# Causal linear attention with 64 heads of width 8: the product of running state and queries in 32 matmuls of two heads instead of 64 of one

## What is computed

```python
xn = _layernorm(x)
q = heads(xn @ Wq.T + bq); k = heads(xn @ Wk.T + bk); v = heads(xn @ Wv.T + bv)
be = jnp.exp(beta)
q = softmax(be * q, axis=-1)
k = softmax(be * k, axis=-1)
kv = jnp.cumsum(jnp.einsum('zsD,zsd->zsDd', k, v), axis=1)
kn = jnp.cumsum(k, axis=1)
num = jnp.einsum('zsD,zsDd->zsd', q, kv)
den = jnp.sum(q * kn, axis=-1, keepdims=True)
attn = (num / den) @ Wo.T + bo
ffn = fp8(clip(xn / input_scale)) * input_scale @ (weight_fp8 * weight_scale).T + bias
out = x + attn + ffn
```

## Time and profile before

| | us |
|---|---|
| median of 3 runs | 1386.97 |
| lowest and highest run | 1383.36 and 1387.37 |
| the profiled execution, device time | 1375.45 |
| its span, first to last instruction | 1373.7 |
| TensorE busy (matmul) | 1224.7 |
| TensorE busy (weight loads) | 731.5 |
| VectorE busy | 1024.7 |
| ScalarE busy | 577.5 |
| GpSimd busy | 321.5 |

### The profile page before, as it was taken

How to read it: one execution, slowest core, us unless ns; L and a number is a source line. 1 busy time by engine, 2 the same in 40 slices (tenths; PEclk the granted TensorE clock), 3 DMA queues, 4 the chain that set the end, 5 groups by cost and what they waited for, 6 DMA issues and landing times.

```text
span 1373.7 us, 81313 instructions
## 1 busy us (share of the span) xinstructions
PE 1224.7 (89%) x36322; PEld 731.5 (53%) x36322; DVE 1024.7 (75%) x2031; ACT 577.5 (42%) x1049; POOL 321.5 (23%) x590
## 2 busy tenths in 40 slices
PE   1569999998999999999999899999999999999995
PEld 1335555555555555555555555555555555555653
DVE  4667778877777887778777777877777877778872
ACT  1534344444444444444444344344344444344431
POOL 3132222222222222222222222221222222122210
PEclk8789999999999999999999999999999999999998
DMA  8022232323323333333333333233233333323321
GB/s 223 10 67 65 75 84 75 82 76 79 75 73 83 70 85 76 81 74 85 76 75 77 76 80 71 77 79 69 76 86 66 76 86 77 75 77 76 69 65 42
DMA packets 181142, 106.01 MB, mean 77 GB/s; under 512 B 120160, under 2 KB 153056, under 8 KB 180832
## 3 DMA queue, kind: packets, MB, share of 16 engines
q1 hardware_dynamic: 180112, 99.79, 30.3%
q10 hardware_dynamic: 720, 1.31, 0.6%
HBM read 40.20 MB, written 16.78 MB: 41 GB/s over the span
## 4 chain that ended last, share of the span: by engine, by line
PE 86%; issue 8%; DVE 2%; DMA 1%; SPq 1%; POOL 0%; ACT 0%; POOLq 0%; DVEq 0%; ACTq 0%
PE s_ps L888 10%; PE a_ps L985 7%; PE a_ps L1004 6%; PE a_ps L905 6%; PE k_ps L861 5%; PE vo_ps L861 5%; PE vo_ps L963 5%; PE vo_ps L863 4%; PE k_ps L865 4%; PE vo_ps L865 4%; PE k_ps L863 4%; PE vo_ps L872 4%; PE vo_ps L874 4%; PE vo_ps L876 4%; PE q_ps L863 4%
## 5 line engine op out<-in xcount | busy, mean ns | idle before, releaser
L507 ACT ACTIVATE q_heads<-qT,cst 128x512 f32<-128x512 f32 x256 | 164.0, 711 | 88.1 <-DVE qT L753 88.1
L400 POOL TENSOR_TENSOR y_sum<-y,y_magic 128x512 f32<-128x512 f32 x64 | 81.4, 1272 | 450.3 <-DVE y_magic L614 450.3
L659 DVE TENSOR_TENSOR att<-s_ps,cst 128x512 f32<-128x512 f32 x256 | 163.8, 681 | 2.1 <-PE s_ps L888 2.1
L393 POOL TENSOR_TENSOR x_split<-xn,x_split 128x512 f16<-128x512 f32 x64 | 74.0, 1157 | 370.6 <-ACT x_split L455 363.4
L498 ACT ACTIVATE q_e<-q_shift,q_exp_scale 128x512 f32<-128x512 f32 x64 | 46.2, 722 | 252.0 <-DVE q_shift L632 252.0
L888 PE MATMUL s_ps<-q_heads,kT 32*32 32x128 f32 x8192 | 148.3, 272 | 2.1 <-issue 1.2
L888 PEld LDWEIGHTS s_ps<-q_heads,kT 32*32 32x32 f32 x8192 | 113.6, 103 | 56.3 <-issue 56.3
L985 PE MATMUL a_ps<-st_seqs,q_heads 128*32 128x36 f32 x8192 | 99.3, 201 | 35.6 <-issue 33.9
L712 DVE TENSOR_TENSOR vp<-vo_ps,vp 128x512 f32<-128x512 f32 x64 | 44.3, 692 | 109.1 <-PE vo_ps L865 109.1
L985 PEld LDWEIGHTS a_ps<-st_seqs,q_heads 128*32 128x32 f32 x8192 | 89.1, 109 | 68.4 <-issue 66.1
L905 PE MATMUL a_ps<-vp,k_e 32*32 32x36 f32 x8064 | 115.0, 198 | 6.4 <-issue 6.3
(11 more groups left out here) (136 smaller groups left out, 2450.4 us busy)
## 6 DMA issues: line engine op xcount, KB each, us to landing
v_groups<-vp SPq DMA_DIRECT2D x1024, 18.0 KB, 2.4
x_in<-L_attn_x SPq DMA_DIRECT2D x64, 256.0 KB
x_res<-L_attn_x SPq DMA_DIRECT2D x64, 256.0 KB
out<-o_sb SPq DMA_DIRECT2D x64, 256.0 KB
w_own<-L_attn_Wk SPq DMA_DIRECT2D x1, 1024.0 KB, 11.4
w_own<-L_attn_Wq SPq DMA_DIRECT2D x1, 1024.0 KB, 13.5
w_own<-L_attn_Wv SPq DMA_DIRECT2D x1, 1024.0 KB, 15.2
att<-L_ffn_weight_fp SPq DMA_DIRECT2D x1, 1024.0 KB, 16.9
```

The costliest lines, as they stand in the source:

```text
L393: gp.tensor_tensor(x_split[:, 1, :], xn[:, :], x_split[:, 0, :], ALU.subtract)\
L400: gp.tensor_tensor(y_sum[:, :], y[:, :], y_magic[:, :], ALU.add).then_inc(ysum_ready, 1)
L507: last = sc.activation(q_heads[:, i.parity, :, j, :], qT[:, :, :], ACT.Copy, scale=head_mask[:, j:j + 1])
L659: v.tensor_tensor(att[:, c, :, :, :].rearrange("p g j s -> p (g j) s"), s_ps[:, DM * (c % 2):DM * (c % 2 + 1)].rearrange("p (h s) -> p h s ...
```

## The change

The inner loop over the four heads of a group takes two at a time. The weights are then 64 columns, two heads side by side, which lie next to each other in `q_heads`, and the result goes to 64 PSUM partitions. The moving operand, the accumulation and the place of every result are as before. The waits are as before too. A step has 32 calls on line 985 instead of 64, and they use two tiles of 64 columns in turn instead of four of 32.

```diff
                     for g in range(G):
-                        for j in range(J):
-                            mm(a_ps[TOK * j:TOK * (j + 1), a_col(g):a_col(g) + GW],
-                               q_heads[:, t.parity, g, j, :], st_seqs[:, t.parity, g, :, :],
+                        for j in range(0, J, 2):
+                            mm(a_ps[TOK * j:TOK * (j + 2), a_col(g):a_col(g) + GW],
+                               q_heads[:, t.parity, g, j:j + 2, :].rearrange("p j s -> p (j s)"),
+                               st_seqs[:, t.parity, g, :, :],
                                start=(g % (G // 2) == 0), stop=False, skip_group_check=True)
```

## The result

| | before | after |
|---|---|---|
| median of the runs side by side, us | 1385.16 (4 runs) | 1325.61 (4 runs) |
| lowest and highest | 1381.10 and 1387.37 | 1323.97 and 1328.23 |
| profiled execution, us | 1375.45 | 1327.04 |
| its span, us | 1373.7 | 1325.2 |
| its mean granted clock | 0.967 | 0.980 |

The ratio is 0.9579, 95% interval 0.9537 to 0.9621: 4.2% faster, where 1.0% was forecast.

The account below looks back on a forecast made before the run. The prediction took TensorE's own queue as the bound. From the profiled 1375.45 us, + 0.7 - 9.1 - 5.0 gave 1362.0 us, 1.0% less, or 1373.5 us carried over to the median; range 1344 to 1400.

Parts of the forecast that it names:

- my case: The whole kernel: 1.0% less time, 4 to 22 us less with terms at their ends; chance 0.56.
- Term 1: Inter product, line 985: half the calls on half the tiles leave array time unchanged at 1.12 us a step; 0.
- Term 2: Weight loads on line 985: 64-column loads stay hidden except the first of each step; +0.7 us, bounds 0 and +22.5.
- The slower rival: Line 985: the 64-column load takes a tile longer than its pass and becomes the bound; up to 1423 us, chance 0.20.
- Term 3: TensorE's issue stops fall in proportion to the 11.3% fewer instruction records; -9.1 us, bounds 0 and -33.9.
- Term 4: Inter product: part of its extra time, from reading beside other engines, goes as fewer streams are read; -5.0 us, bounds 0 and -10.0.
- Term 5: Stages behind the inter product: VectorE takes up earlier data at once, other engines' queues are untouched and cost nothing.
- hang on the number of passes: Rival, inter product: pass count sets the pace, so halving passes saves 35.8 to 54.4 us plus stops; 1332 to 1342, chance 0.10.
- Nothing measurable: Rival, whole kernel: stops are tied to time or transfers, not program, and the disturbance stays; 1387.5 us carried over, chance 0.14.

Follow-up runs that it names:

- e2: The changed kernel with 18 instead of 36 moving columns on line 985, half of the sequences left out; 1324.07 us.
- e8: The kernel before with 18 instead of 36 moving columns on line 985, half of the sequences left out; 1382.77 us.
- e3: The changed kernel with 64 tiny matmuls added to every step ahead of the intra product; 1448.49 us.
- e13: The changed kernel with 64 tiny matmuls ahead of the intra product in the first step only; 1314.42 us, ratio 0.9553 to the kernel before.
- e5: The kernel before with half of the scores left out; 1337.22 us.
- e4: The kernel before with heads 1 and 3 of each group left out of the inter product; 1281.21 us.
- e7: The kernel before with its inter product split in two halves, ahead of and behind the output projection, one head a call; 1329.54 us, ratio 0.967.
- e1: The kernel before with all four heads of a group in one inter-product call of 128 weight columns; 1424.28 us, ratio 1.0265.

## Why the prediction was wrong

**Direction right, by other amounts.** The forecast was 1.0% less on the sum 0 + 0.7 - 9.1 - 5.0 = -13.4 us. In the profiled executions it is -48.4, made of +33, -63 and -20, the first two each well outside the bounds that I gave them. The sentence that my case "with its terms at their ends" gives 4 to 22 us less was wrong as a sum: the bounds of the terms add up to +22.5 and -43.9 us, and the measured -48.4 lies outside them too.

**Term 1, array time 0.** What failed is its premise, "what sets the pace is the moving columns of each tile's passes". The pace is set by the slower of two things. For the scores, with 128 moving columns to 32 weight columns, it is indeed the moving ones: 112 ns. For the inter product it is the load after the change (e2), and before it the moving columns don't set it either (e8). 36 moving columns at 0.84 ns and 32 weight columns at 0.8 ns come to nearly the same, so the rows of one shape fitted either reading, and I took the one that left the change free.

**Term 2, loads +0.7 us, at most +22.5.** It measured +33.2 us of busy time, +49 us against the undisturbed pace of the old stage. The step that failed is "0.34 ns a column", from the load records of the transposes beside those of line 985. They are loads of another kind of call, one record a call where the matmul has two. On line 985's own calls 32, 64 and 128 columns have records of 109, 138 and 193 ns, 0.9 ns a column. The 22 ns for 64 columns are 58. The Trainium skill, page "TensorE: Matmul & The Clock Gate", section "LDWEIGHTS (loading the stationary operand)", gives a load of P columns P / 1.2 ns, which makes 27, 53 and 107 ns for 32, 64 and 128; the passes here took 33, 58 and 111, so it was right within 6 ns, and "the trace speaks against the rule" was wrong. The slower rival named the mechanism, the load as the bound, and its place. That its 22 ns more a pass come close to the measured 58.2 - 35 = 23 is luck: they were a load of 22 ns put behind a pass, and the load takes some 58 ns with the pass inside it (e2). Its time, 1411 to 1423 us, failed by the stops.

**Term 3, stops -9.1 us, at most -33.9.** It measured -63.3. That the stops are late program was right (e3, e13, and the packets of the queue). The step that failed is that they "come with the amount of program that is read": 11.3% less program alone is worth at most some 18 us (e5, 17.7), and some 45 go with the dense run that became shorter. The bound failed too, since I let only line 985's own stops fall, and those of lines 1004, 863 and 865 fell with it: one dense run, several lines. The dense run had 536 entries in (1.3 + 2.6 + 1.3) = 5.2 us, over two blocks of 256. Now it has 408 in 2.06 + 2.6 + 1.3 = 6.0 us. That the slower stage also gives the supply time is at most a small part of it: e4 has 408 entries in 1.23 + 2.6 + 1.3 = 5.1 us and only 4.1 us of waits more, and e3 keeps the slow stage and has 82.9. The Trainium skill, page "Runtime: NRT & Kernel Launch", section "Instruction fetch mechanics", calls the cost of a block's end mostly hidden. Here 81.0 us of 1373.7 were not. Its block of 16 KiB agrees with the 256.0 entries between the places of the long stops.

**Missing from the sum: the clock.** After 11 of 21 long stops the clock is at 1.2 GHz for some 3.4 us. It was in the windows of the kernel before and would have been a term of 1.5 to 1.7 us for each such stretch taken away, 18.8 us in all. It brought most of the -19.9.

**Term 4, the disturbance -5.0 us.** The disturbance was real and went whole. The old stage took 99.3 us against 83 of its own pace, 12 of the 16 in short pauses; the changed one takes 132.5 against 64 x 2.06 = 131.8. In the total it can't be read as a term of its own, since the +33.2 contains it. The cause given, reading beside the transfers, does not fit: with half the moving columns the old stage varied as before (e8), and in e7's second half the same one-head calls stand at the same place, at a mean DMA share of 0.84 against 0.63 in the old stage, and 51 of 61 groups last 0.77 us exactly. What makes the pauses stays open, and no run took away the transfers alone.

**Term 5** held. VectorE's waits for the two products fell from 109.1 to 91.7 and from 59.6 to 42.8 us, and it didn't become the bound.

**The other rivals.** The pace does not hang on the number of passes (e4: half of them in nearly the same time, 1.23 us for 64 against 1.30 for 128, because they use half the tiles); that this rival's 1332 to 1342 us came nearest to the 1325.61 is luck. "Nothing measurable" was wrong, since the stops are tied to the program.

## What to carry to other kernels

Where TensorE has "issue" waits in the middle of equal passes, count program entries along the order of the work: a long run of many small passes, broken only by short stretches of large matmuls, pays for it. Here 536 entries in 5 or 6 us had 63 to 84 us of waits, 472 had 38 and 408 had 10 to 36; the limit between them will be another in another kernel. The cure is to spread the runs (e7, not one call changed, 3.3%) or thin them out. A stop is worth its length and, in about half of the long ones here, the clock after it.

For a pass of a float32 call on a tile, an estimate from the scores (112 ns), e4, e2 and e1, within 3 ns of each, is the larger of weight columns and moving columns at 0.83 ns each and some 5 ns: making weights wider pays only while they stay below the moving side. Take such a price from rows of the same kind of call.

## What the runs showed of the hardware that I had not expected

- Two column tiles of 64 load side by side: starts are 29.1 ns apart, a load of one tile takes 58.2.
- Stops move when the program is shifted by 128 entries (line 905: 6.4 to 0.7 us), with everything else the same, and the kernel is 9.5 us faster (4.6 in the profiled executions).
- The long stops stand a multiple of 256.0 entries apart, over 1200 us without an exception, and end 1.20 to 1.60 us behind a packet of program.
- After a stop of 2.01 us the granted clock was 0.50, for about 3 us of fully busy array; 11 of 21 long stops had this, and one of 2.52 us did not.
- A stage that loses 33 us of its own time can leave the kernel 48 us faster.
